# First attention pass of a graph kernel: logits between the groups of the attending, exponential and parts of a diffusion in its middle

## What is computed

```python
def _top_p_attention(X, W1, W2, W3):
    q = X @ W1.T @ W2.T
    k = X @ W3.T
    probs = softmax(q @ k.T)
    idx = argsort(-probs)
    sp = take_along_axis(probs, idx)
    cs = cumsum(sp)
    keep_sorted = cs - sp < 0.9
    mask = zeros(probs.shape, bool).at[rows, idx].set(keep_sorted)
    A = probs * mask
    return A / maximum(A.sum(-1, keepdims=True), 1e-12)

R = S + eye(N); R = R / R.sum(-1)          # S is the adjacency
Xf = X; Xa = X
for n in range(2):
    A = _top_p_attention(Xa, W1, W2, W3)
    Xf = R @ Xf
    Xa = A @ Xa
    Z = Z + Xf @ U1[n].T + Xa @ U2[n].T
```

## Time and profile before

| | us |
|---|---|
| median of 3 runs | 7123.94 (7119.68 to 7130.17) |
| profiled execution | 7131.35 |
| its span | 7129.6 |
| VectorE busy | 5314.4 (75%) |
| TensorE busy | 4537.1 (64%) |
| ScalarE busy | 2161.8 (30%) |
| mean granted TensorE clock | 0.828 of full |

### The profile page before, as it was taken

How to read it: one execution, slowest core, us unless ns; L and a number is a source line. 1 busy time by engine, 2 the same in 40 slices (tenths; PEclk the granted TensorE clock), 3 DMA queues, 4 the chain that set the end, 5 groups by cost and what they waited for, 6 DMA issues and landing times. The chain is left out here.

```text
span 7129.6 us, 80171 instructions
## 1 busy us (share of the span) xinstructions
PE 4537.1 (64%) x27812; PEld 3255.7 (46%) x27812; DVE 5314.4 (75%) x13021; ACT 2161.8 (30%) x3033; POOL 344.0 (5%) x170
## 2 busy tenths in 40 slices
PE   5995688888665364523475588553337888835981
PEld 2442467676554354522464477453311222205981
DVE  4885577777448888887888899886349999974864
ACT  2332565656311011100132244222132222213541
POOL 0000000000110000000000000010000222020000
PEclk9997788888897787866787799786669999977995
DMA  5551000000032122111111122110103333303840
GB/s 171 202 199 57 1 2 1 1 1 1 21 132 97 57 86 85 75 40 43 58 66 57 50 87 93 59 58 17 29 16 130 107 110 109 110 26 144 292 161 29
DMA packets 192671, 549.28 MB, mean 77 GB/s; under 512 B 20027, under 2 KB 77126, under 8 KB 192126
## 3 DMA queue, kind: packets, MB, share of 16 engines
q1 hardware_dynamic: 187069, 539.58, 21.2%
q0 software_dynamic: 5120, 3.97, 0.2%
HBM read 526.73 MB, written 16.68 MB: 76 GB/s over the span
## 5 line engine op out<-in xcount | busy, mean ns | idle before, releaser
L655 PE MATMUL ps<-ident,arena 125*125 125x125 f32 x3200 | 562.9, 311 | 1161.4 <-DVEq L1139 1161.4
L655 PEld LDWEIGHTS ps<-ident,arena 125*125 125x125 f32 x3200 | 492.9, 224 | 1201.7 <-DVEq L1139 1201.7
L687 PE MATMUL ps<-arena 125*125 125x129 f32 x6400 | 834.5, 289 | 308.9 <-DMA arena<-in_adj_tiles 301.1
L663 PE MATMUL ps<-arena,turned 125*125 125x129 f32 x6400 | 943.7, 297 | 104.7 <-ACT turned L759 104.7
L1438 DVE SCALAR_TENSOR_TENSOR arena<-arena,pair 125x1000 f32<-125x1000 f32 x800 | 939.3, 1253 | 71.3 <-ACT arena L1401 71.3
L759 ACT ACTIVATE turned<-ps 125x500 f32<-125x500 f32 x800 | 464.4, 587 | 1699.4 <-PE ps L655 1698.2
L687 PEld LDWEIGHTS ps<-arena 125*125 125x125 f32 x6400 | 782.5, 199 | 380.6 <-DMA arena<-in_adj_tiles 298.1
L663 PEld LDWEIGHTS ps<-arena,turned 125*125 125x125 f32 x6400 | 869.3, 208 | 121.3 <-ACT turned L759 117.6
L1456 PE MATMUL ps<-arena 125*64 125x500 f32 x3200 | 765.0, 601 | 192.9 <-DVE arena L1438 192.8
L1092 DVE SCALAR_TENSOR_TENSOR arena<-arena,wt 125x5000 f32<-125x5000 f32 x80 | 434.1, 5427 | 194.6 <-issue 194.6
L1456 PEld LDWEIGHTS ps<-arena 125*64 125x64 f32 x3200 | 197.9, 137 | 756.9 <-DVE arena L1438 525.1
(11 more groups left out here) (343 smaller groups left out, 6073.1 us busy)
## 6 DMA issues: line engine op xcount, KB each, us to landing
arena<-in_adj_wide SPq DMA_DIRECT2D x400, 500.0 KB, 4.5
arena<-in_adj_tiles SPq DMA_DIRECT2D x400, 488.3 KB
arena<-in_adj_wide SPq DMA_DIRECT2D x100, 1000.0 KB, 4.8
x_saved<-arena SPq DMA_DIRECT2D x4, 2500.0 KB
arena<-x_saved SPq DMA_DIRECT2D x3, 2500.0 KB
arena<-att_saved SPq DMA_DIRECT2D x1, 2519.5 KB
arena<-in_x SPq DMA_DIRECT2D x1, 2500.0 KB
arena<-in_h SPq DMA_DIRECT2D x1, 2500.0 KB
```

The costliest lines, as they stand in the source:

```text
L655: mm = pe.transpose(banks_turn[:, g % 2, c * P:(c + 1) * P], work[b % DEPTH][:, j:j + P], ident[0:P, 0:P])
L663: mm = pe.matmul(acc_attend, turned[:, g % 2, c * P:(c + 1) * P], nodes(v_attend, FA)[:, j, :], start=(j == 0), stop=(j == NB - 1))
L687: mm = pe.matmul(acc_spread, ring[:, j * P:(j + 1) * P], values[:, j, :], start=(j == 0), stop=False)
```

## The change

In the first pass, for blocks 1 to 37, TensorE puts one group of `logits(b + 2)` behind each group of `attend(b - 1)`, and ScalarE copies them between its own copies. Behind group 5 (`HALFWAY`) ScalarE does `exponentials(b + 1)`, and TensorE two or three pieces of a diffusion (`SPREAD_PIECES`, 100 pieces in all, so 20 diffusions). The semaphores of the diffusion are now made once for both passes, and the second pass begins with diffusion 20; its list has 60. VectorE puts `highest` into the first `settle` after the last chunk of maxima, in both passes (`owed`). The second pass is not woven.

```diff
+HALFWAY = 5
+SPREAD_FIRST = 20
+SPREAD_PIECES = [2, 3] * 20
-SPREADS = (5, 3, [4] * 8 + [0, 3, 3] + [1, 1, 2, 1] * 6 + [2, 2, 0, 0, 0])
+SPREADS = (5, 3, [4, 4, 4, 0] + [4] * 4 + [1, 1, 1, 0] * 8)
...
-                    def attend(b):
+                    def attend(b, beside=None, halfway=()):
                         pe.wait_ge(s_kept, b + 1)
                         pe.wait_ge(s_out, b + 1)
                         turn(b, 0)
...
                             if g + 1 < NG:
                                 turn(b, g + 1)
                             multiply(b, g)
+                            if beside is not None:
+                                logit(beside, g)
+                            if g == HALFWAY:
+                                for n in halfway:
+                                    diffuse_piece(n // PIECES, n % PIECES)
...
+                        woven = not arranged and 0 < b < NB - 2
                         if b > 0:
-                            attend(b - 1)
-                        if b + 2 < NB:
+                            attend(b - 1, b + 2 if woven else None, pieces_in(b) if pieces else ())
+                        elif pieces:
+                            for n in pieces_in(b):
+                                diffuse_piece(n // PIECES, n % PIECES)
+                        if b + 2 < NB and not woven:
                             logits(b + 2)
...
-                    def take(b):
+                    def take(b, beside=None):
                         for g in range(NG):
...
                             a.activation(turned[:, g % 2, :], banks_turn[:, g % 2, :], ACT.Copy)\
                              .then_inc(s_taken, 1)
+                            if beside is not None and g > 0:
+                                copy_logit(beside, g - 1)
+                            if beside is not None and g == HALFWAY:
+                                exponentials(beside - 1)
+                        if beside is not None:
+                            copy_logit(beside, NG - 1)
                         a.wait_ge(s_used, (b + 1) * NG)
...
                             v.wait_ge(s_link, ahead["links"])
                         else:
                             v.drain()
+                            if ahead["owed"]:
+                                highest(ahead["par"])
+                                ahead["owed"] = False
...
                         search(u)
-                        if more_blocks:
+                        if ahead["owed"]:
                             highest((u + 1) % DEPTH)
+                            ahead["owed"] = False
...
-            attention_step("s0", VA, VB, STEPS[0:6], 1, 2 * P)
+            attention_step("s0", VA, VB, STEPS[0:6], 1, 2 * P, pieces=SPREAD_PIECES)
```

More of the change, by code:

```diff
@@ L523, in _, with attention_step @@
                     v.drain()
-        def attention_step(name, v_attend, raw_attend, steps, rounds, span, spreads=(), arranged=False):
+        loaded = [ctx.enter_context(nc.semaphore(f"adjacency_loaded{q}")) for q in range(PIECES)]
+        s_spread, s_diffused, s_diff_kept = (ctx.enter_context(nc.semaphore("adjacency_" + n))
+                                             for n in ("spread", "diffused", "diff_kept"))
+        def attention_step(name, v_attend, raw_attend, steps, rounds, span, spreads=(), pieces=(), arranged=False):
             with ExitStack() as c1:
@@ L539, in attention_step @@
                     chosen_in = [sem(f"chosen_in{k}") for k in range(DEPTH)]
+                if pieces:
+                    pieces_in = lambda b: range(sum(pieces[:b]), sum(pieces[:b + 1]))
+                    ended_in = lambda b: [n // PIECES for n in pieces_in(b) if n % PIECES == PIECES - 1]
                 if spreads:
-                    loaded = [sem(f"loaded{q}") for q in range(PIECES)]
-                    s_spread, s_diffused, s_diff_kept = sem("spread"), sem("diffused"), sem("diff_kept")
                     s_scaled = sem("scaled")
                     ahead_of_logits, ahead_of_blocks, per_block = spreads
+                    ahead_of_logits += SPREAD_FIRST
                     first_in = [ahead_of_logits + ahead_of_blocks + sum(per_block[:b]) for b in range(NB + 1)]
@@ L597, in _ @@
                     if spreads:
-                        for n in range(ahead_of_logits):
+                        for n in range(SPREAD_FIRST, ahead_of_logits):
                             adjacency(n)
@@ L604, in _ @@
                         for n in range(ahead_of_logits, first_in[0]):
+                            adjacency(n)
+                    if pieces:
+                        for n in range(SPREAD_FIRST):
                             adjacency(n)
@@ L642, in _, with logit @@
                 def _(pe):
+                    def logit(b, g):
+                        if g == 0:
+                            pe.wait_ge(s_query, 2 * b + 2)
+                        pe.wait_ge(s_copied, (b if g >= 4 else b - 1) * NG + freed[g] + 1 + NG)
+                        pe.matmul(bank_logit[g % 4], query[b % DEPTH][g % 2], keys_at(g),
+                                  start=True, stop=True).then_inc(s_logit, 1)
                     def logits(b):
-                        pe.wait_ge(s_query, 2 * b + 2)
                         for g in range(NG):
-                            pe.wait_ge(s_copied, (b if g >= 4 else b - 1) * NG + freed[g] + 1 + NG)
-                            pe.matmul(bank_logit[g % 4], query[b % DEPTH][g % 2], keys_at(g),
-                                      start=True, stop=True).then_inc(s_logit, 1)
+                            logit(b, g)
                     def turn(b, g):
@@ L674, in attend, with diffuse_piece, diffuse @@
                             multiply(b, g)
-                    def diffuse(n):
+                            if beside is not None:
[3 more added lines that the diff above has]
+                                    diffuse_piece(n // PIECES, n % PIECES)
+                    def diffuse_piece(n, q):
                         r = n % NB
                         values = nodes(spread_from[n // NB], FA)
-                        if n == NB:
+                        if n == NB and q == 0:
                             pe.wait_ge(s_scaled, 1)
-                        if n:
+                        if n and q == 0:
                             pe.wait_ge(s_diff_kept, n)
-                        for q in range(PIECES):
[L684 to L692, removed]
+                        pe.wait_ge(loaded[q], 16 * n + 16)
+                        for c in range(PC):
+                            j = q * PC + c
+                            mm = pe.matmul(acc_spread, ring[:, j * P:(j + 1) * P], values[:, j, :],
+                                           start=(j == 0), stop=False)
+                        mm.then_inc(s_spread, 1)
+                        if q == PIECES - 1:
+                            pe.matmul(acc_spread, ident[0:P, 0:P], values[:, r, :],
+                                      start=False, stop=True).then_inc(s_diffused, 1)
+                    def diffuse(n):
+                        for q in range(PIECES):
+                            diffuse_piece(n, q)
                     def turn_query(b):
@@ L738, in set_query, with copy_logit @@
                             a.activation(query[b % DEPTH][half], source, ACT.Copy).then_inc(s_query, 1)
+                    def copy_logit(b, g):
+                        a.wait_ge(s_logit, b * NG + g + 1)
+                        a.activation(work[b % DEPTH][:, g * GW:(g + 1) * GW], bank_logit[g % 4],
+                                     ACT.Copy).then_inc(s_copied, 1)
                     def copy_logits(b):
                         for g in range(NG):
[L742 to L744 removed]
+                            copy_logit(b, g)
                     def exponentials(b):
@@ L783, in _ @@
                             set_query(b + 2)
+                        woven = not arranged and 0 < b < NB - 2
                         if b > 0:
-                            take(b - 1)
-                        if b + 2 < NB:
+                            take(b - 1, b + 2 if woven else None)
+                        if pieces:
+                            for n in ended_in(b):
+                                keep_diffused(n)
+                        if b + 2 < NB and not woven:
                             copy_logits(b + 2)
-                        if b + 1 < NB:
+                        if b + 1 < NB and not woven:
                             exponentials(b + 1)
@@ L821, in _ @@
                     CHUNKS = N // span
-                    ahead = {"par": 0, "next": CHUNKS, "links": 0}
+                    ahead = {"par": 0, "next": CHUNKS, "links": 0, "owed": False}
                     def one_maximum():
@@ L1113, in step @@
                         v.sem_clear(s_link)
-                        ahead.update(par=(u + 1) % DEPTH, next=0 if more_blocks else CHUNKS, links=0)
```

(2 more changed lines are left out.)

2 lines of the change are left out of this document (1 added, 1 removed).

## The result

| | before | after |
|---|---|---|
| median, us | 7123.26 (7119.68 to 7130.17) | 7285.02 (7283.31 to 7287.6) |
| ratio | | 1.0226 (95% interval 1.0208 to 1.0244) |
| span of the profiled execution | 7129.6 | 7281.6 |
| first pass, first step to last result | 1098.5 | 1261.7 |
| a block of it, mean of 37 | 27.30 | 31.75 |

The kernel became 2.3% slower where 0.6% faster was forecast. Of the 152.0 us that the span grew, the first pass has 163.2; the second gave back 4.0 and the stages around them 7.2.

The account below looks back on a forecast made before the run. The first pass was taken as a circle of attending, logits and exponential with neither VectorE nor TensorE full. 7131.35 - 56 - 5 + 16 = 7086, or 7079 for the median; 7065 to 7095 at 50%, whole range 7038 to 7112.

Parts of the forecast that it names:

- VectorE's wait for the exponential: First pass: VectorE waits 4.50 us a block for the next block's exponential; the change was to bring this near zero.
- the later loop: First pass: TensorE and ScalarE at 24.5 us a block at full clock, about 25.3 at the expected clock, against VectorE's 24.4.
- the 0.96 of the sum: TensorE's granted clock assumed for the new first pass, taken from dense second-pass blocks; it makes 24.5 us about 25.3.
- the diffusion covers the exponential: First pass: diffusion pieces of 3.6 or 5.5 us run during the exponential, where TensorE would otherwise stand about 4 us.
- Part 1: First pass: exponential into the middle of the attending, logits between its groups; 954 us against 1010, 56 less.
- 0.42 where no bank is short: First pass, TensorE: price in us of a group of logits, giving 1.74 for a woven group with 1.32 of attending.
- upper bound: First pass, TensorE: most a group of logits was taken to cost, 0.53 us, from ten in 5.27.
- The rivals: Four other outcomes: clock full 7043 (20%), clock halved 7220 (8%), milder halving 7103 (13%), no change 7125 to 7135 (5%).
- The slower one: First pass: TensorE falls to half clock each block through small idles, 29.6 us a block, 7220; 8% with cases near it.
- VectorE's loop: First pass: VectorE alone needs 24.4 us a block on average, and 29.0 in three blocks where its program turns over.
- Part 2: Twenty diffusions move from second pass to first: 5 us less from one VectorE wait; the rest, 0 to 20, taken as 0.
- Part 3: Second pass: the earlier maximum leaves its place beside the branch and costs 39 x 0.41, 16 us more; ends 0 and 19.

Follow-up runs that it names:

- experiment 3: The kernel before, not woven, with keys of groups 0 to 4 in the lower half of the rows and 5 to 9 in the upper; 7199.92 us.
- experiment 1: The changed kernel with two groups of logits behind every second group of the attending, not one behind each; 7112.88 us.
- experiment 2: The kernel with pairs of logits groups, keys laid out so four pairs of five lie in one half of the rows; 7204.38 us.
- experiment 9: The changed kernel with paired logits, diffusion pieces 2, 2, 1, late maximum in the second pass, and ring loads held until VectorE's masking is done; 7043.12 us.
- experiment 8: The changed kernel with the maximum put back behind the search in the second pass; 7275.93 us.
- experiment 5: The kernel with pairs of logits groups, but all 80 diffusions in the second pass again and none in the first; 7133.85 us.

## Why the prediction was wrong

**Right**: VectorE's wait for the exponential went; TensorE and ScalarE became the later loop; the clock rose, and to 0.99, above the 0.96 of the sum; the diffusion covers the exponential; loads are never waited for.

**The step that failed** is the price of a group of logits in Part 1, "0.42 where no bank is short". It was read off two rows of weight loads that are 0.42 apart and count two loads each. A group has two loads and two products (20 products for ten groups), and I took the two loads of a row for one group's. They were one load of each of two neighbouring groups: a pair takes 0.84. A rate measured in a pair was used as the price of a group alone, and its "upper bound" of 0.53 came from the same paired stage and so bounded nothing. The runs give the parts:

| | us |
|---|---|
| one group alone, no change of kind (experiment 3) | 0.84 |
| one group alone, woven (changed kernel: 2.55 - 1.32) | 1.23 |
| two groups in both halves, woven (experiment 1: 2.55 - 1.32) | 1.23 |
| two groups in one half, woven (experiment 2: 3.38 - 1.32) | 2.06 |

So a change to logits (64 rows, 500 columns) from the attending (125 rows, 129 columns) and back costs 0.39, a group alone 0.84 beside that, and a second group in the other half nothing more. Of the 0.81 by which the term was too small for each group, 0.42 is the lost neighbour and 0.39 the change of kind, of which the sum had no term at all. Ten groups are 8.1 a block: 24.5 + 8.1 = 32.6, less some 1.1 that TensorE no longer stands at the exponential, is 31.5; measured are 30.5 and 32.4 in turn, and 31.75 on average. With the right term the same sum would have given a slower kernel: 31.5 - 27.3 in 37 blocks is 155 us more in the first pass, where 163.2 were measured. Whether the 0.39 comes from the rows or from the columns of the products was not tested apart.

**The rivals** all dealt with the clock or with the exponential. The slower one was right in its sign and wrong in its mechanism; the section of the Trainium skill on small idles between groups (TensorE: Matmul & The Clock Gate, A second HAM failure mode: psum-queue depth-cycling), which was named beside it, is not borne out here: the clock is at 0.99, though the ten groups of each block go through the four banks. The section that did bear on the change is the one named under experiment 2.

**VectorE's loop** was priced at 24.4, and at 29.0 where its program turns over. The changed kernel doesn't show it, since TensorE is later. In experiment 9 the mean is 25.34, and the first two turns of the loop take 28.6 and 28.5; the third doesn't stand out. The eight longer gaps at the branch came as forecast, 3.5 to 3.6 without loads (3.3 in the forecast), but up to 6.9 with loads, a term that the sum didn't have.

**Part 2** (5 less, and 0 taken for the rest of up to 20): 16.5 less by experiment 8, 20.2 by experiments 1 and 5. The one wait of 5 went as said (33.0 for 37.5 in that block). A further 2.6 is the turn of VectorE's loop, at which the step began after 3.79 and not 6.38; most of the rest lies in five of the long blocks, 1 to 3 each, and was not traced further. **Part 3** (16 more): 12.5 or 17.0, by experiments 8 and 5. The two together came to 4.0 less where 11 more was forecast.

## What to carry to other kernels

A product that uses half of the array's rows is half of a pair: before it is moved, see which neighbour it runs beside, and move the two together. A rate read from a stage of alternating instructions holds for that stage alone; count whose loads and products a merged row holds before taking it as the price of one. When a wait is removed, what it had covered (here the instruction gaps of VectorE) comes to the front, and loads put into that stretch can lengthen it.

## What the runs showed of the hardware

- Two fp32 groups of logits (64 rows and 500 columns, two products each) take 1.04 us on TensorE when their operands lie in different halves of the rows, 1.87 when they lie in one; a lone group takes as long as a pair.
- A change from products with 125 rows and 129 columns to ones with 64 rows and 500 columns, and back, costs TensorE 0.39 us at full clock beside the products themselves.
- Work put into a gap made TensorE quicker: with a gap of 2.65 us in each block the clock was 0.88, with pieces of diffusion in it 0.98, and the block was 26.88 with 4.6 us more of work and 27.10 without.
- In 8 of 38 blocks VectorE's gap ahead of the masking is 3.5 to 3.6 us and holds a fetch of 8 KB of instructions; in most others it is 1.2 to 1.3. With data loads under way the fetch starts 4.1 to 5.0 us into the gap and not 1.7, and the gap is 6.0 to 6.9. Delaying the loads by part of a block gave 29 us.
